# A fused attention and expert kernel: six reorderings of its startup, of a one-tile unit and of one step of its tail

## The reference

```
xn = layernorm(x)
q, k, v = xn Wq^T + bq, xn Wk^T + bk, xn Wv^T + bv
theta = 0.5 + 0.2 sigmoid(q k^T) + 0.15 tanh(q k^T) + 0.1 relu(q k^T)
s = (softmax(theta) v) Wo^T + bo
e = argmax(softmax(xn Wr + br))                  # one of 8 experts per token
y = gelu(xn W1[e] + b1[e]) W2[e] + b2[e]         # 256 -> 1024 -> 256
out = x + s * silu(y)
```

## Time and profile before

| | |
|---|---|
| median of 3 runs | 527.48 us (527.33 to 527.98) |
| the profiled execution's own time | 527.64 us |
| its span, first to last instruction | 525.6 us |
| TensorE busy | 515.6 us, 98% |
| VectorE busy | 402.6 us, 77% |
| ScalarE busy | 344.6 us, 66% |
| GpSimd busy | 195.8 us, 37% |
| chain that ended last, by engine | PE 86%, ACT 6%, DVE 5%, issue, POOL and DMA 1% each |

### The profile page before, as it was taken

One profiled execution on the slowest core, in us unless ns is written; L12 is line 12 of the kernel. 1 busy time (PEld: TensorE's weight loads), 2 busy tenths in 40 slices (PEclk: granted clock), 3 DMA queues, 4 the chain that ended last, 5 costly groups with the idle time before them and its releaser, 6 DMA issues.

```text
span 525.6 us, 10829 instructions
## 1 busy us (share of the span) xinstructions
PE 515.6 (98%) x3773; PEld 484.3 (92%) x3773; DVE 402.6 (77%) x811; ACT 344.6 (66%) x633; POOL 195.8 (37%) x227
## 2 busy tenths in 40 slices
PE   7999999999999999999999989999999999999997
PEld 6899998899989999899999979998999989999997
DVE  5898689946578855598555688768999998867887
ACT  4789778437356733466343575899787786777884
POOL 3218419913112222222112222005676785342441
PEclk9999999999999999999999999999999999999999
DMA  8964720031635711247311421005233232211221
GB/s 266 344 225 176 285 81 1 2 120 32 230 123 151 255 55 41 61 133 237 112 40 40 136 70 42 21 22 190 62 99 113 71 114 87 62 44 49 60 71 51
DMA packets 40754, 57.49 MB, mean 109 GB/s; under 512 B 3654, under 2 KB 35788, under 8 KB 40156
## 3 DMA queue, kind: packets, MB, share of 16 engines
q1 hardware_dynamic: 35452, 46.02, 26.5%
q0 software_dynamic: 3488, 9.47, 6.4%
q10 hardware_dynamic: 1760, 1.32, 0.8%
HBM read 41.07 MB, written 17.56 MB: 112 GB/s over the span
## 4 chain that ended last, share of the span: by engine, by line
PE 86%; ACT 6%; DVE 5%; issue 1%; POOL 1%; DMA 1%; ACTq 0%; DVEq 0%
PE ps L899 26%; PE ps L901 25%; PE ps L900 25%; PE ps L1014 5%; DVE stats L1375 2%; PE ps L1193 1%; PE ps L1080 1%; ACT hid L763 1%; POOL xn_all L464 1%; DMA xn_all<-in_L_attn_x_dram 1%; PE ps L1070 1%; ACT relu_s L628 1%; ACT tanh_s L625 1%; ACT theta L624 1%; PE ps L1045 1%
## 5 line engine op out<-in xcount | busy, mean ns | idle before, releaser
L899 PE MATMUL ps<-v_hi,pT_hi 128*128 128x258 f32 x256 | 74.9, 293 | 0.2
L747 ACT ACTIVATE hid<-ps,b_now 128x256 f32<-128x256 f32 x128 | 53.7, 472 | 29.7 <-PE ps L901 28.8
L900 PE MATMUL ps<-v_lo,pT_hi 128*128 128x258 f32 x256 | 72.5, 283 | 0.0
L901 PE MATMUL ps<-v_hi,pT_lo 128*128 128x258 f32 x256 | 72.3, 282 | 0.0
L1430 DVE SCALAR_TENSOR_TENSOR theta<-tanh_s,theta 128x512 f32<-128x512 f32 x64 | 47.3, 739 | 23.5 <-ACT tanh_s L625 22.9
L899 PE MATMUL ps<-w_hi_even,hidT_h 128*128 128x256 f32 x200 | 58.5, 293 | 1.6 <-DVE hidT_l L1727 1.1
L636 ACT ACTIVATE theta<-theta,neg_max 128x512 f32<-128x512 f32 x64 | 43.0, 720 | 24.9 <-DVE neg_max L1436 24.6
L519 POOL COPY unit_token<-sorted_token 128x2 int32 x19 | 4.5, 238 | 142.9 <-PE ps L1193 142.9
L901 PE MATMUL ps<-w_hi_even,hidT_l 128*128 128x256 f32 x200 | 56.6, 283 | 0.0
L900 PE MATMUL ps<-w_lo_even,hidT_h 128*128 128x256 f32 x200 | 56.6, 283 | 0.0
L778 ACT ACTIVATE g_sb<-y_sb 128x512 f32<-128x512 f32 x20 | 12.6, 631 | 65.8 <-DVE y_sb L1742 65.8
(11 more groups left out here) (258 smaller groups left out, 1641.5 us busy)
## 6 DMA issues: line engine op xcount, KB each, us to landing
w_raw_odd<-in_L_ffn_W_dram SPq DMA_DIRECT2D x10, 1024.0 KB
w_raw_even<-in_L_ffn_W_dram SPq DMA_DIRECT2D x6, 1024.0 KB
sorted_g<-g_sb SPq DMA_DIRECT2D x20, 256.0 KB, 2.2
xn_rows<-xn_all SPq DMA_DIRECT2D x4, 1024.0 KB, 6.2
x_tile<-in_L_attn_x_dram SPq DMA_DIRECT2D x32, 128.0 KB, 2.2
out_dram<-g_tile SPq DMA_DIRECT2D x32, 128.0 KB, 1.7
xn_all<-in_L_attn_x_dram SPq DMA_DIRECT2D x3, 1024.0 KB, 12.4
kept_xT<-passing_xT SPq DMA_DIRECT2D x2, 1024.0 KB, 4.0
```

The source lines that it names most:

```text
L747: last = nc.scalar.activation(hid[:, j % 2, c * UNIT:(c + 1) * UNIT], ps[:, HID_BANK + j, c * UNIT:(c + 1) * UNIT], ACT.Gelu, bias=b1_now[ ...
L899: mm(dst, a_hi, b_hi, start=first, stop=False)
L900: mm(dst, a_hi, b_lo, start=False, stop=False)
L901: return mm(dst, a_lo, b_hi, start=False, stop=last)
```

## The change

It has six edits. (1) Of batch 0's first four tiles, ScalarE normalizes one instead of two and VectorE two instead of one. (2) ScalarE and VectorE choose a half unit by an else branch instead of a second comparison. (3) TensorE forms the four products of G before it routes the tokens of tiles 4 to 7, instead of mixed with them. (4) VectorE takes the row statistics of two tiles ahead of the first half of `thetas(0)` and of two more behind it, instead of two behind it; the rest of the row statistics of that batch are taken later, as before. (5) In a half unit, VectorE's `low_w1` of the next expert stands behind step s = 1 instead of in front of all steps. (6) In the tail, for n = 10 alone (`TPB + 2`), TensorE runs `weighted(9)` ahead of `transposes(10)` and `job(10)`.

```diff
--- before.py
+++ after.py
@@ -660,7 +660,7 @@
 
             square_root(0, slice(0, 4))
             act.wait_ge(scales_ready, 1)
-            normalize(range(2))
+            normalize(range(1))
             for m in range(DC):
                 high_M(m)
             high_xT_0(0)
@@ -801,7 +801,7 @@
                     gelus(u0, par)
                     row_high(u0 + 1)
                     high_w1(w1_landed, other, raw[0], slice(0, 1))
-                with act.If(full < u0 + 1):
+                with act.Else():
                     gelus_half(u0, par, beside=lambda: high_w1(w1_landed, other, raw[0], slice(0, 1)))
                     row_high(u0 + 1)
                 high_w1(w1_landed, other, raw[0], slice(1, 2))
@@ -1122,9 +1122,9 @@
                 for ec in range(DC):
                     last = mm(ps[:, 7, m * D:(m + 1) * D], wv_raw[:, ec, m * P:(m + 1) * P], woT[:, ec, :],
                               start=ec == 0, stop=ec == DC - 1)
-                    if m == DC - 1 and ec == DC - 1:
-                        last.then_inc(G_done, 1)
-                    route_0(4 + 2 * m + ec)
+            last.then_inc(G_done, 1)
+            for t in range(4, TPB):
+                route_0(t)
             for ec in range(DC):
                 last = mm(ps[:, PT_BANK, 0:D], bv_wide[:, ec, :], woT[:, ec, :], start=ec == 0, stop=ec == DC - 1)
             last.then_inc(const_done, 1)
@@ -1341,6 +1341,10 @@
                     wait_apart(pe, y_biased, end_of[E - 1])
                     weighted(n - 1)
                     transposes(n)
+                elif n == TPB + 2:
+                    weighted(n - 1)
+                    transposes(n)
+                    job(n)
                 else:
                     pe.wait_ge(pT_ready, n * 2)
                     transposes(n)
@@ -1495,7 +1499,7 @@
             variances(0, 4)
             scales(0, 0, 4)
             dve.wait_ge(scales_ready, 1)
-            normalize(range(2, 3))
+            normalize(range(1, 3))
             dve.wait_ge(x0_in[1], 16)
             statistics = row_statistics(range(4, TPB))
             dve.wait_ge(biasT_done, 1)
@@ -1567,9 +1571,10 @@
                 take_logits(now, source)
                 score_offsets(i, now, source[:, :, E])
 
-            thetas(0, [0])
             dve.wait_ge(x_in[2], 16)
             row_statistics(range(2 * TPB, 2 * TPB + 2))
+            thetas(0, [0])
+            row_statistics(range(2 * TPB + 2, 2 * TPB + 4))
             dve.wait_ge(G_high, 1)
             v.tensor_tensor(G_lo[:, :, :], pair_of(ps[:, 7, :]), G_hi[:, :, :].bitcast(F32), ALU.subtract
                             ).then_inc(G_ready, 1)
@@ -1584,7 +1589,7 @@
             dve.wait_ge(bo_halved, 1)
             v.scalar_tensor_tensor(attn_const[:, :], ps[:, PT_BANK, 0:D], 0.5, bo_all[:, :], ALU.mult, ALU.add
                                    ).then_inc(const_kept, 1)
-            row_statistics(range(2 * TPB + 2, 3 * TPB))
+            row_statistics(range(2 * TPB + 4, 3 * TPB))
             dve.wait_ge(x_in[1], 16)
             step(row_statistics(range(TPB, 2 * TPB)))
             variances(TPB, 3 * TPB)
@@ -1713,8 +1718,6 @@
 
                 dve.wait_ge(hid_done, u * 4 + 2)
                 v.tensor_copy(hid[:, 1, :], ps[:, HID_BANK + 1, :]).then_inc(dve_kept, 1)
-                if beside:
-                    beside()
                 first = half_gelus(0)
                 for c in range(2):
                     now = slice(c, c + 1)
@@ -1735,6 +1738,8 @@
                         dve.wait_ge(hidT_copied, u * 4 + 3)
                     v.tensor_tensor(hidT_l[:, now, 0:P], gelu, hidT_h[:, now, 0:P].bitcast(F32), ALU.subtract
                                     ).then_inc(hidT_ready, 1)
+                    if s == 1 and beside:
+                        beside()
                 dve.sem_inc(hidT_copied, 1)
 
             def biased(u, par):
@@ -1758,7 +1763,7 @@
                     hidden_parts(u)
                     row_low(u + 1)
                     low_w1(e, other, 0)
-                with dve.If(full < u + 1):
+                with dve.Else():
                     parts_half(u, beside=lambda: low_w1(e, other, 0))
                     row_low(u + 1)
                 low_w1(e, other, 1)
```

## The result

| | before | changed |
|---|---|---|
| median | 527.55 us (527.16 to 527.98, 6 runs) | 530.18 us (529.43 to 531.03, 6 runs) |
| profiled execution | 527.64, span 525.6 | 530.45, span 528.7 |
| around the span | 2.04 | 1.75 |

What follows compares the result with a forecast made beforehand. It took TensorE, 98% busy, as the bound. Tail +1.47, half unit -0.25, first tiles +0.17 and batch 0 -0.16 gave +1.23 us, so 528.7 us was forecast, range 527.8 to 529.2.

Steps and rivals of the forecast that it cites:

- the largest term: Tail: weighted(9), put first, waits for the PSUM bank that finish(8) frees; +1.47 us.
- the sum: All terms together: tail +1.47, half unit -0.25, first tiles +0.17, batch 0 -0.16, giving +1.23 us.
- the half unit: Else branch and moved split: TensorE starts 1.0 us earlier, then waits anew for step 2's parts; -0.25 us net.
- rival (d): Tail: TensorE's clock falls in the new wait, costing 5.2 us more up to scores(12), 533.9 us; chance 0.03.
- my case: The main forecast of 528.7 us, with its own range of 528.2 to 529.2; chance 0.72.
- The first tiles: Startup: transposes start 0.3 us earlier, but VectorE's second tile delays the bias copy and TensorE restarts; +0.17 us.
- Edit 6 by itself: Tail's new order: TensorE's wait for the bank and restart, 2.67 us in place of 1.21; +1.47 taken.
- The break-even at 359.7: Tail: the new order gains only if finish(8) frees the bank before 359.7; it was expected at 361.17.
- Rival (a): Tail: if the bank is free when TensorE asks, the order gives -1.21 us, 526.0 us in all; chance 0.07.
- Batch 0: Statistics order and products of G: the reciprocal starts 0.11 us earlier, G up to 0.06 earlier; -0.16 us.
- (b): Half unit: it gives its whole 1.0 us because the split hides beside TensorE's four columns; 528.0 us; chance 0.10.
- (c): First tiles: they keep their 0.3 us because something other than the bias copy holds TensorE; 528.2 us; chance 0.08.

Runs made afterwards that it cites:

- x3: The changed kernel with ten small matmuls of unused result on TensorE in the wait ahead of weighted(9): 529.15 us, ratio 1.0027.
- x1: The kernel before with only the tail's new order, weighted(9) ahead of transposes(10) and job(10): 530.27 us, ratio 1.0041.
- x6: The kernel before with only VectorE's low_w1 split in the half unit moved behind step s = 1; the If stays: 528.01 us, one execution.
- x7: The kernel before with only the half unit's second If replaced by an Else on ScalarE and VectorE: 527.43 us, one execution.
- x5: The changed kernel with finish(8) on VectorE moved between transposed_parts(9) and job(9): 527.69 us, ratio 1.0004.
- x4: The changed kernel with finish(8) on VectorE moved between the two halves of thetas(10): 527.14 us, ratio 0.9989.
- x8: The kernel before with edits 3 to 6 and finish(8) between the halves of thetas(10); old first tiles, no Else: 526.64 us, ratio 0.9984.

## Why the prediction was wrong

The sign and the largest term were right, the size was not. The median came out 530.18 - 528.7 = 1.5 us above the forecast. In the profiled execution the last matmul stands +3.10 later, 1.87 more than the +1.23 of the sum: 1.57 are the clock, 0.32 the half unit, 0.06 the stages up to 121 (+0.07 there without the rows' -0.08, forecast +0.01), and the rows' -0.08 is the rest. With the idle time filled (x3) the median is 529.15, inside my range.

**The clock, rival (d), +1.57 where it falls.** This is the step that failed: the sum had the wait's length and nothing for TensorE's speed behind it. I had a chance of 0.03 for the fall, on the ground that waits up to 1.10 had shown none. (Rows 2 don't reach the half unit's 1.10; the trace has 1.00 there too.) No row of the kernel before has a wait near 2.5 us, so those rows said nothing on one. It fell in four of six executions here and in three of five of x1. I had also priced it apart from my case, at 5.2 us, by letting the lower level last to `scores(12)`. It lasted 3.4 us, all of it within `weighted(9)`, and cost 1.57 in the profiled executions. Between the executions of one kernel with and without it the difference is less: 1.03 in the changed kernel (530.48 to 529.45), 0.80 in x1 (530.32 to 529.52). The Trainium skill's page TensorE: Matmul & The Clock Gate, section "What's actually happening", says that an idle array falls back. The profiled execution agrees (0.51 behind 2.42 idle); four executions of eleven with the same wait show no such fall.

**The half unit, +0.07 instead of -0.25.** Up to 321 the step was right, even a little short: -0.33, with the new wait where I had put it and TensorE back at 312.06, not 312.17. Each of the two edits has about half of it (x6 -0.15, x7 -0.18). But I had followed it to the end of the unit only. The next unit waits for the gate's product on VectorE, and that for ScalarE's tanh, which starts no earlier. The gain turned into a wait there, and the pause of ScalarE's register loads made it +0.07.

**The first tiles, +0.37 instead of +0.17 at 12 us** (+0.29 without the rows' -0.08). I priced VectorE's second tile at 0.33, by the distance from the first to what followed. It took 0.50 (7.95 to 8.78 for two, against 0.33 for one): the first tile of VectorE took 0.41, the second 0.58. The likely reason, which no run isolates, is GpSimd's tile, which began at 8.02, between VectorE's two, and ended at 8.71. The bias products then paid 0.10 for the restart (1.09 against 0.99), as reckoned. By 121 the 0.37 and batch 0's part had come to +0.07, so about 0.1 is given back in and behind batch 0. That the sum of both (+0.01 forecast) came out nearly right is partly luck.

**What was right.** Edit 6 by itself, without the clock: +1.47 forecast, +1.45 measured in x3. The break-even at 359.7: x5. Rival (a)'s condition: with the bank free the order wins, 0.72 to 0.94 in the traces rather than 1.21, since TensorE then waits for the parts of tile 10. Batch 0: -0.16 forecast, -0.13 to -0.20 from 43 to 62 in the kernels that have it. Rivals (b) and (c) did not come.

What stays open: in the executions whose mean clock shows no fall the changed kernel (529.45) is still 0.3 above x3, and x1 (529.33 and 529.71) 1.9 above before, where the wait alone is 1.45; no trace shows one of them. Open too is what brings ScalarE's pause.

## What to carry to other kernels

Before TensorE's order is changed, look up who frees the bank that the earlier product writes: with the releaser moved on VectorE the tail's new order gave 0.72 to 0.94 us (x4, x8), without that it took 1.45 (x3), or 3.0 where the clock fell (x1). A wait longer than any in the trace before is not covered by its clock rows: price the lower level inside the forecast, with a chance of its own (here it fell in seven executions of eleven). And follow a gain to the next place where the waiting engine meets a chain that did not start earlier.

## What the runs showed of the hardware

The granted clock fell behind a wait of 2.4 us in seven of eleven executions by their mean clock (in the two with a trace to 0.5, for 3.4 us), and did not fall so behind 1.05 us in any of ten (x5), nor in any of nine where the wait was filled with small matmuls (x3). In the two traces the fall began after TensorE had started again, 0.1 us behind in x1 and 0.9 in the changed kernel, not in the idle time. What decides whether it falls, the runs don't show.

Some of VectorE's instructions took longer where one of GpSimd's had begun before them: a normalized tile 0.58 instead of 0.41, the relu step 1.11 to 1.25 instead of 0.69. Where VectorE had begun first, its relu step kept 0.69 and GpSimd's product took 1.07 instead of 0.73 (the kernel before, at 361.81). The Trainium skill's page SBUF — State Buffer, section "Who interferes with whom", says that the two engines share a pair of ports, that whoever issues first has it for the whole instruction, and that the other is blocked. The traces agree: the second tile, too, ended 0.15 after GpSimd's (8.86 and 8.71).
